# Width-8 attention: scores and shifted scores as paired 64-row tiles

## The chip, the cores and the metric

The kernel runs on one core of a Trainium2 chip. The metric is the device time of one execution in microseconds. TensorE multiplies matrices, VectorE and ScalarE work on what it leaves in PSUM, GpSimd works on SBUF alone, and SyncE issues the DMAs.

## The reference

A network of four layers on x of 16 batches x 256 tokens x 128 features. Each layer adds an attention and then a feed-forward part, each on a layer norm of x. Three of the parts are attentions with 16 heads of width 8, and only they are touched here: the attention of layer 1, the four experts of layer 2's feed-forward part, and the rotary attention of layer 3. Cut to what matters:

```python
# layer 1: 16 batches, one set of weights
q, k, v = split(x @ W_qkv + b_qkv)               # heads of width 8
attn = softmax(einsum('bqhe,bkhe->bqhk', q, k)) / sqrt(128)
x = x + einsum('bihv,bvhd->bihd', attn, v) @ W_out + b_out
# layer 2, for each of 4 experts: keys of tokens that the router
# did not give to the expert are masked, the result is gated
att = softmax(where(valid, einsum('bqhd,bkhd->bhqk', q, k) * 0.5, -1e9))
out += gate[e] * ((att @ v) @ wo[e] + bo[e])
# layer 3: q and k turned by a rotary table, scores * 8 ** -0.5
```

## The kernel before, in words

`attention8` (L287) does one such attention. A *job* is one batch with one set of weights: 16 jobs in layer 1 (stage a1), 64 in layer 2 (a2, masked, four experts per batch), 16 in layer 3 (a3, rotary). The stages between them (layer norms, the 64-wide attention of layer 0, feed-forward parts, a Fourier attention) are not touched.

Queries and keys of a job are projected in float32 and split into three bfloat16 parts each; the parts are written to a scratch in DRAM and read back as *stacks*: for each head a column of 48 rows (six products of parts) in `stackq` and `stackk`, so that one bfloat16 matmul gives the float32-like score. Row 64 carries the mask, rows 96 and 97 the negated row maximum, as two bfloat16 parts.

Each head is computed twice. `scores` (L435) contracts 65 rows and gives query x key; VectorE takes the row maxima (`maxima`, L627). The maxima are negated and split on GpSimd (`split_max`), transposed on TensorE (`turn_max`), copied by ScalarE (`copy_max`) and sent by DMA into the stack (`max_rows`), in two halves of eight heads. `shifted` (L447) then contracts 98 rows and gives key x query less the maximum; ScalarE takes the exponential (`exponential`, L557), and `prob_values` (L460) multiplies with the values, four heads side by side in 32-column tiles, in float32. The result has a column of ones for the denominator; it is copied, transposed (`turn_output`), divided on VectorE (`normalise`), transposed again (`turn_y`) and projected (`project_out`).

All engines run the same software pipeline (`pipeline`, L276): a *step* has 16 slots, one per head, and in the step of job n, TensorE does the scores of job n+1 and the shifted scores of job n, slot by slot; projections for job n+3 stand at the end of the step. Both kinds of score have two PSUM banks each (`psS`, `psT`), so that a head waits for the maximum or the exponential of two heads before. Two more banks are shared in turn by everything else, in the order that `misc_uses` gives. The order on each engine is that of its `step` function. SyncE's DMAs stand in one queue in program order.

```python
for t in range(2):                                   # scores, L443
    mm = pe.matmul(psS[h % 2][:, t * SEQ:(t + 1) * SEQ], stackq[0:MASK_ROW + 1, b, h, t * P:(t + 1) * P],
                   stackk[0:MASK_ROW + 1, b, h, :], start=True, stop=True)
```

The 64-wide attention (L806 on) is not changed, but it has score matmuls of two heads at `tile_position=(64 * h, 0)`, each on 64 rows of the array (L822, L826).

## Time and profile before

| | |
|---|---|
| median of 3 runs | 2939.5 us (2938.18 to 2943.69) |
| the profiled execution | 2944.34 us, span 2942.6 us |
| TensorE busy | 2582.3 us (88%) |
| VectorE, ScalarE, GpSimd busy | 1958.5, 1577.3, 490.1 us |
| mean granted TensorE clock | 0.934 |
| stages a1, a2, a3 | about 700 to 980, 1320 to 2410, 2450 to 2740 us |
| values, 128x256, VectorE (L638) | 425 ns, x96 |
| x with gate, 128x128, VectorE (L659) | 346 ns for most, two per job |
| statistics, VectorE (L114) | 283 ns, two per batch |
| maxima on GpSimd, 128x16 (L730, L732, L734) | 252, 217, 252 ns, each twice per job |
| parts on GpSimd, 128x512 (L720, L722) | 610, 1156 ns, each once per job |

The engines' busy times overlap; each share is of the span. A matmul's duration in the timeline contains its way through the array: where matmuls follow each other, the distance between their starts is what each costs. A float32 product is in the records as two matmuls, and "x16" counts records. A line in the DMA queue's timeline is the issue of a DMA, not its transfer.

### The profile page before, as it was taken

What the parts mean: (1) busy time and instruction counts of PE and PEld (TensorE: products, weight loads), DVE (VectorE), ACT (ScalarE), POOL (GpSimd) and SP (SyncE); (2) the same over time, 40 slices, a digit from 0 to 9 for tenths busy, and PEclk for the clock granted to TensorE, in tenths of its full rate; (3) what the DMA queues carried; (4) which work ended last, traced back from release to release, by engine and by line L of the source; (5) the groups of instructions that cost most, each with busy time, mean ns of one, the idle gap of its engine ahead of it and who ended that gap; (6) DMA issues with size and microseconds to landing.
All of it is one profiled execution on the core that took longest, in us unless ns stands there. A gap on an engine that the chain in (4) does not pass through costs nothing. (4 is left out here: it accounts for less than half of the span.)

```text
span 2942.6 us, 71873 instructions
## 1 busy us (share of the span) xinstructions
PE 2582.3 (88%) x21177; PEld 1696.7 (58%) x21177; DVE 1958.5 (67%) x4869; ACT 1577.3 (54%) x3823; POOL 490.1 (17%) x1071
## 2 busy tenths in 40 slices
PE   5999999796999776649999999999999977999798
PEld 3777777553666444426666666666666644666454
DVE  6666666645878457737787777877778755888211
ACT  2555555423777422226777776777777753666310
POOL 2111111101221000002221222222222203332000
PEclk9999999996999887758999999999999987999899
DMA  4000000001322000002222222222222202222001
GB/s 128 1 0 0 0 0 0 1 1 44 77 70 72 1 1 0 0 17 76 73 72 71 71 75 69 71 73 71 72 71 71 75 25 62 70 66 66 1 0 29
DMA packets 123330, 128.37 MB, mean 44 GB/s; under 512 B 17402, under 2 KB 102222, under 8 KB 123215
## 3 DMA queue, kind: packets, MB, share of 16 engines
q1 hardware_dynamic: 123214, 126.94, 16.0%
q8 instruction: 60, 0.98, 0.1%
q14 instruction: 56, 0.45, 0.1%
HBM read 85.36 MB, written 39.88 MB: 43 GB/s over the span
## 5 line engine op out<-in xcount | busy, mean ns | idle before, releaser
L631 DVE TENSOR_REDUCE a_rowmax<-a_psS 128x2 f32<-128x512 f32 x1536 | 996.0, 685 | 303.9 <-PE a_psS L443 284.1
L561 ACT ACTIVATE a_probs<-a_psT 128x512 f32<-128x512 f32 x1536 | 882.4, 595 | 332.5 <-PE a_psT L455 305.2
L443 PE MATMUL a_psS<-stackk,stackq 65*128 65x256 bf16 x3072 | 607.8, 280 | 103.8 <-DMA stackk<-mask_dram 54.9
L455 PE MATMUL a_psT<-stackq,stackk 98*128 98x256 bf16 x3072 | 593.6, 275 | 14.3 <-ACT a_probs L561 4.7
L443 PEld LDWEIGHTS a_psS<-stackk,stackq 65*128 65x128 bf16 x3072 | 237.2, 98 | 335.0 <-DVE a_rowmax L631 180.2
L469 PE MATMUL a_psO<-a_probs,values 128*32 128x256 f32 x6144 | 414.5, 388 | 0.0
L455 PEld LDWEIGHTS a_psT<-stackq,stackk 98*128 98x128 bf16 x3072 | 275.9, 98 | 115.1 <-ACT a_probs L561 54.0
L893 ACT ACTIVATE a_probs<-a_psS,a_negmax 128x256 f32<-128x256 f32 x256 | 121.2, 473 | 257.0 <-DVE a_negmax L917 257.0
L469 PEld LDWEIGHTS a_psO<-a_probs,values 128*32 128x32 f32 x6144 | 161.0, 109 | 148.3 <-issue 72.1
L730 POOL TENSOR_SCALAR a_negmax<-a_rowmax 128x16 bf16<-128x16 f32 x192 | 48.5, 252 | 984.5 <-DVE a_rowmax L631 982.7
L569 ACT ACTIVATE a_oT<-a_psO 128x256 f32<-128x256 f32 x384 | 145.6, 379 | 46.2 <-PE a_psO L469 46.2
L220 PE MATMUL n_turned<-identity,n_xn 128*128 128x128 f32 x256 | 70.0, 433 | 101.3 <-DVE n_xn L195 98.7
L478 PE MATMUL a_shared<-identity,a_oT 128*128 128x128 f32 x768 | 147.5, 273 | 4.4 <-ACT a_oT L569 4.4
L800 POOL TENSOR_TENSOR a_vr<-a_v,a_rsum 128x256 f32<-128x256 f32 x128 | 78.4, 612 | 372.3 <-DVE a_rsum L927 372.3
L575 ACT ACTIVATE a_negmaxT<-a_shared 16x256 bf16<-16x256 bf16 x192 | 71.5, 372 | 104.5 <-PE a_shared L485 99.0
L1098 DVE TENSOR_SCALAR mlp_h<-mlp_b,s 128x512 f32<-128x512 f32 x32 | 24.0, 751 | 140.3 <-PE mlp_b L1067 86.0
L220 PEld LDWEIGHTS n_turned<-identity,n_xn 128*128 128x128 f32 x256 | 45.7, 217 | 123.7 <-DVE n_xn L195 87.7
L1067 PE MATMUL mlp_b<-mlp_h,k 128*128 128x512 f32 x256 | 114.6, 592 | 0.0
L722 POOL TENSOR_TENSOR a_parts<-a_rest,a_parts 128x512 bf16<-128x512 f32 x96 | 111.0, 1156 | 17.8 <-POOL a_parts L720 17.8
L916 DVE TENSOR_REDUCE a_negmax<-a_psS 128x1 f32<-128x256 f32 x256 | 107.5, 420 | 5.7 <-issue 3.9
L927 DVE RECIPROCAL a_rsum<-a_sums 128x4 f32<-128x4 f32 x128 | 22.8, 178 | 127.0 <-ACT a_probs L895 127.0
L478 PEld LDWEIGHTS a_shared<-identity,a_oT 128*128 128x128 f32 x768 | 94.9, 140 | 13.0 <-ACT a_oT L569 7.2
(192 smaller groups left out, 4140.4 us busy)
## 6 DMA issues: line engine op xcount, KB each, us to landing
a_scratch<-a_parts SPq DMA_DIRECT2D x96, 384.0 KB, 2.8
stackq<-a_scratch SPq DMA_DIRECT2D x192, 96.0 KB
stackk<-a_scratch SPq DMA_DIRECT2D x192, 96.0 KB
stackq<-a_scratch SPq DMA_DIRECT2D x192, 64.0 KB
stackk<-a_scratch SPq DMA_DIRECT2D x192, 64.0 KB
stackq<-a_scratch SPq DMA_DIRECT2D x192, 32.0 KB
stackk<-a_scratch SPq DMA_DIRECT2D x192, 32.0 KB
stackq<-a_negmaxT SPq DMA_DIRECT2D x384, 4.0 KB
```

Source lines behind the costliest of these rows:

```text
L220: t = pe.transpose(turned[b][:, k * D:(k + 1) * D], xn[:, b, k, :], m.identity[:, :])
L443: mm = pe.matmul(psS[h % 2][:, t * SEQ:(t + 1) * SEQ], stackq[0:MASK_ROW + 1, b, h, t * P:(t + 1) * P], stackk[0:MASK_ROW + 1, b, h, :], s ...
L455: mm = pe.matmul(psT[h % 2][:, t * SEQ:(t + 1) * SEQ], stackk[0:MAX_ROW + 2, b, h, t * P:(t + 1) * P], stackq[0:MAX_ROW + 2, b, h, :], sta ...
L469: mm = pe.matmul(psO[g % 2][SLOT * j:SLOT * (j + 1), 0:SEQ], values[:, s.parity(off), t, 4 * g + j, :], probs[:, g % 2, j, t * SEQ:(t + 1) ...
L478: mm = pe.transpose(ps[:, t * P:(t + 1) * P], oT[:, g % 2, t * P:(t + 1) * P], m.identity[:, :])
L561: act.activation(probs[:, h // 4 % 2, h % 4, :], psT[h % 2][:, :], ACT.Exp, scale=w.exp_scale).then_inc(exp_done, 1)
L569: act.activation(oT[:, g % 2, :], psO[g % 2][:, 0:SEQ], ACT.Copy).then_inc(oT_ready, 1)
L631: dve.tensor_reduce(rowmax[:, s.parity(1), h, :], psS[h % 2][:, :].rearrange("p (t k) -> p t k", t=2), AX_X, ALU.max).then_inc(max_done, 1)
L722: pool.tensor_tensor(parts[:, :, 2, :], rest[:, :, :], parts[:, :, 1, :], ALU.subtract).then_inc(parts_ready, 1)
L893: act.activation(probs[:, a, h, 0:SEQ], psS[a][h][:, 0:SEQ], ACT.Exp, bias=negmax[:, a, 2 * h:2 * h + 1], accum_out=sums[:, a, 2 * h:2 * h ...
L916: dve.tensor_reduce(negmax[:, a, 2 * h:2 * h + 1], psS[a][h][:, 0:SEQ], AX_X, ALU.max, negate=True)
L1067: mm = pe.matmul(banks1[c % 2][:, :], w.k1[:, k, c * P:(c + 1) * P], h0[:, s.parity(0), k, :], start=(k == 0), stop=(k == CH - 1))
```

## The change

The stacks of a head now take 51 of 64 rows (48, the mask, two of the maximum), and heads 0-3 and 8-11 lie on rows 0 to 63, the others on rows 64 to 127. So a score matmul uses one half of the array's rows, and the shifted matmul issued beside it is of a head in the other half: in unit u of a step TensorE does head u's scores of job n+1 and the shifted scores of head u+4 of job n-1 (or head u-12 of job n), which are 28 units behind their scores. One wait for both engines stands ahead of the four matmuls.

The maxima of all 16 heads are split, transposed, copied and sent at once, by two DMAs. The stacks are held for four jobs (before: two) and loaded by twelve DMAs, of eight heads each, queries ahead of the maxima and keys behind them; the mask row is one DMA for both groups. The probabilities of all 16 heads are kept; the values are placed so that two blocks of four heads add into one PSUM bank, in columns 0-8 and 9-17 of a head's 32, and there are two output copies and four output transposes per job in place of four and eight. Queries and keys are copied out of PSUM by ScalarE with their bias; GpSimd does the whole split, and in the rotary attention the two products with the table as well, which VectorE did before. The pipeline starts one step earlier and ends one step later.

```diff
 HEADS = 16
 HD = 8
 SLOT = 32
-BF_ROWS = 48
-MASK_ROW = 64
-MAX_ROW = 96
+PAIRS = HEADS // 2
+GROUP_ROWS = 64
+MASK_ROW = 48
+MAX_ROW = 49
+ZERO_ROW = 51
+LEAD = 4
 EXPERTS = 4
...
+    jobs, unroll, first = BATCHES * weights, 4, 4
+    plan = Plan(jobs, weights, unroll, first, rounds=(jobs - LEAD - first) // unroll, drain=2)
+    plan.misc_uses = [("qk", 3)] + ([("qk2", 3)] if rotary else []) + [("o", -2), ("m", 0), ("y", -2), ("out", -2), ("v", 0)]
...
+        def place(h):
+            return h // 4 % 2, 4 * (h // 8) + h % 4
+        def shifted_head(u):
+            return (-1, u + 4) if u < 12 else (0, u - 12)
...
+            def max_rows(s):
+                wait_taken_alone(sp, s, "m", 0, sp_passed)
+                if s.known(0, 1):
+                    wait_alone(sp, shifted_ready, s.n(0, HEADS), sp_passed)
+                for g in range(2):
+                    r = GROUP_ROWS * g + MAX_ROW
+                    sp.dma_start(stackq[r:r + 2, s.quarter(0), :, :], negmaxT[HEADS * g:HEADS * (g + 1), :]).then_inc(maxrow_ready, 16)
+            def save(s):
+                wait_alone(sp, parts_ready, s.n(3, 1, 1), sp_passed)
+                if s.known(3, 2):
+                    wait_alone(sp, stack_ready, s.n(2, stack_inc), sp_passed)
+                sp.dma_start(scratch[s.parity(3)].rearrange("qk part p t -> p qk part t"),
+                             parts[:, :, :, :]).then_inc(parts_saved, 16)
+            def stacks(s, qk):
+                b = s.quarter(2)
+                if qk == 0:
+                    wait_alone(sp, parts_saved, s.n(2, 16, 16), sp_passed)
+                    if s.known(2, 1):
+                        wait_alone(sp, stack_ready, s.n(2, stack_inc), sp_passed)
+                    if s.known(2, 4):
+                        wait_alone(sp, shifted_ready, s.n(-2, HEADS, HEADS), sp_passed)
+                src = scratch[s.parity(2)].rearrange("qk part (g d h) t -> qk part g d h t", g=2, h=PAIRS)
+                for g in range(2):
+                    for repeats, part, row in ((3, 0, 0), (2, 1, 24), (1, 2, 40)):
+                        rows = slice(GROUP_ROWS * g + row, GROUP_ROWS * g + row + 8 * repeats)
+                        if qk == 0:
+                            sp.dma_start(stackq[rows, b, :, :], src[0, part, g, :, :, :].unsqueeze(0).to_broadcast([repeats, HD, PAIRS, SEQ])).then_inc(stack_ready, 16)
+                        else:
+                            sp.dma_start(stackk[rows, b, :, :], src[1, 0:repeats, g, :, :, :]).then_inc(stack_ready, 16)
+                if masked and qk == 1:
                     row = m.mask_dram[s.batch(2), s.expert(2)]
+                    sp.dma_start(stackk[MASK_ROW:P:GROUP_ROWS, b, :, :],
+                                 row.unsqueeze(0).unsqueeze(0).to_broadcast([2, PAIRS, SEQ])).then_inc(stack_ready, 16)
+            def step(s):
+                if s.has(2):
+                    stacks(s, 0)
                 if s.has(0):
+                    max_rows(s)
                 if s.has(2):
+                    stacks(s, 1)
+                if s.has(3):
+                    save(s)
...
+            def scores_part(s, u, t):
+                i, pr = place(u)
+                r, b = GROUP_ROWS * i, s.quarter(1)
+                return pe.matmul(psS[u % 2][:, t * SEQ:(t + 1) * SEQ], stackq[r:r + MAX_ROW, b, pr, t * P:(t + 1) * P],
+                                 stackk[r:r + MAX_ROW, b, pr, :], start=True, stop=True, tile_position=(r, 0))
+            def shifted_part(s, u, t):
+                off, h = shifted_head(u)
+                i, pr = place(h)
+                r, b = GROUP_ROWS * i, s.quarter(off)
+                return pe.matmul(psT[u % 2][:, t * SEQ:(t + 1) * SEQ], stackk[r:r + ZERO_ROW, b, pr, t * P:(t + 1) * P],
+                                 stackq[r:r + ZERO_ROW, b, pr, :], start=True, stop=True, tile_position=(r, 0))
+            def score_pair(s, u):
+                off, h = shifted_head(u)
+                if s.has(1):
+                    if u == 0:
+                        pe.wait_ge(stack_ready, s.n(1, stack_inc, stack_inc))
+                    if s.known(1, 1) or u >= 2:
+                        pe.wait_ge(max_done, s.n(1, HEADS, u - 1))
+                if s.has(off):
+                    if h == 0:
+                        pe.wait_ge(maxrow_ready, s.n(0, 32, 32))
+                    if s.known(off, 1) or h >= 2:
+                        pe.wait_ge(exp_done, s.n(off, HEADS, h - 1))
                 for t in range(2):
+                    if s.has(1):
+                        a = scores_part(s, u, t)
+                        if t == 1:
+                            a.then_inc(scores_ready, 1)
+                    if s.has(off):
+                        b = shifted_part(s, u, t)
+                        if t == 1:
+                            b.then_inc(shifted_ready, 1)
+            def prob_values(s, k):
+                half, i = k // 2, k % 2
+                if k == 0:
+                    wait_taken(pe, s, "v", -1)
+                pe.wait_ge(exp_done, s.n(-1, HEADS, 4 * k + 4))
+                if i == 0 and s.known(-1, 1):
+                    pe.wait_ge(oT_ready, s.n(-1, 2, half - 1))
                 for t in range(2):
                     for j in range(4):
+                        mm = pe.matmul(psO[half][SLOT * j:SLOT * (j + 1), 0:SEQ], values[:, s.parity(-1), t, 8 * i + 4 * half + j, :],
+                                       probs[:, 4 * k + j, t * SEQ:(t + 1) * SEQ], start=(t == 0 and i == 0), stop=(t == 1 and i == 1),
                                        tile_position=(0, SLOT * j), skip_group_check=True)
                 mm.then_inc(pv_ready, 1)
...
+            def turn_output(s):
+                pe.wait_ge(oT_ready, s.n(-2, 2, 2))
+                ps, full = fill(s, "o", -2)
                 for t in range(2):
+                    for half in range(2):
+                        c = (2 * t + half) * P
+                        mm = pe.transpose(ps[:, c:c + P], oT[:, half, t * P:(t + 1) * P], m.identity[:, :])
...
+                for u in range(HEADS):
+                    score_pair(s, u)
+                    if u == 0 and s.has(3):
                         project_qk(s, "qk", w.wq, w.wk)
                         if rotary:
                             project_qk(s, "qk2", w.wq2, w.wk2)
+                    if u == 2 and s.has(-2):
+                        turn_output(s)
+                    if u % 4 == 3 and s.has(-1):
+                        prob_values(s, u // 4)
+                    if u == 4 and s.has(0):
+                        turn_max(s)
+                    if u == 6 and s.has(-2):
+                        turn_y(s)
+                    if u == 9 and s.has(-2):
+                        project_out(s)
+                    if u == 12 and s.has(0):
+                        project_v(s)
...
+            def copy_qk(s, kind, which):
+                ps, taken = wait_full(act, s, kind, 3)
+                if which == 0 and s.known(3, 1):
+                    if rotary:
+                        act.wait_ge(turned_ready, s.n(3, 3))
+                    else:
+                        act.wait_ge(rest_ready, s.n(3))
+                e = s.expert(3)
+                for k in range(2):
+                    bias = w.rot_bias[:, 2 * which + k:2 * which + k + 1] if rotary else (w.bq, w.bk)[k][:, e:e + 1]
+                    c = act.activation(raw[:, which, k, :], ps[:, k * SEQ:(k + 1) * SEQ], ACT.Identity, bias=bias)
+                c.then_inc(taken, 1)
+            def exponential(s, u):
+                off, h = shifted_head(u)
+                if not s.has(off):
+                    return
+                act.wait_ge(shifted_ready, s.n(off, HEADS, h + 1))
+                if h % 4 == 0 and s.known(off, 1):
+                    act.wait_ge(pv_ready, s.n(off, 4, h // 4 - 3))
+                act.activation(probs[:, h, :], psT[u % 2][:, :], ACT.Exp, scale=w.exp_scale).then_inc(exp_done, 1)
...
+                for u in range(HEADS):
+                    if u == 0 and s.has(-2):
+                        copy_oT(s, -2, 1)
+                    if u == 5 and s.has(0):
+                        copy_max(s)
+                    if u == 7 and s.has(-2):
                         copy_yT(s)
+                    exponential(s, u)
+                    if u == 1 and s.has(3):
+                        copy_qk(s, "qk", 0)
+                        if rotary:
+                            copy_qk(s, "qk2", 1)
+                    if u == 8 and s.has(-1):
+                        copy_oT(s, -1, 0)
...
+            def normalise(s):
+                ps, taken = wait_full(dve, s, "o", -2)
+                if s.known(-2, 1):
+                    wait_taken(dve, s, "y", -3)
+                o = ps[:, :].rearrange("p (t h c) -> p t h c", t=2, c=SLOT)
+                for i in range(2):
+                    r = dve.reciprocal(rden[:, i, :, :], o[:, :, :, 9 * i + HD])
+                r.then_inc(rden_ready, 1)
+                dve.wait_ge(rden_ready, s.n(-2, 1, 1))
+                for i in range(2):
+                    of = slice(D // 2 * i, D // 2 * (i + 1))
+                    u = dve.tensor_tensor(y[:, :, of].rearrange("p t (h d) -> p t h d", d=HD), o[:, :, :, 9 * i:9 * i + HD],
+                                          rden[:, i, :, :].unsqueeze(3).to_broadcast([P, 2, 8, HD]), ALU.mult)
+                u.then_inc(taken, 1)
...
+                    if u == 3 and s.has(-2):
+                        normalise(s)
+                    if u == 10 and s.has(-2):
+                        add_output(s)
+                    if u == 11 and s.has(-2) and s.expert(-2) == weights - 1:
+                        output_stats(s)
+                    if u == 13 and s.has(0):
                         write_values(s)
...
+            def turn(s):
+                for which in range(2):
+                    wait_taken_alone(pool, s, ("qk", "qk2")[which], 3, pool_passed)
+                    pool.tensor_tensor(raw[:, which, :, :], raw[:, which, :, :], w.tables[:, which, :, :], ALU.mult).then_inc(turned_ready, 1)
+                wait_alone(pool, turned_ready, s.n(3, 3, 2), pool_passed)
+                if s.known(3, 1):
+                    wait_alone(pool, rest_ready, s.n(3), pool_passed)
+                pool.tensor_tensor(turned[:, :, :], raw[:, 0, :, :], raw[:, 1, :, :], ALU.add).then_inc(turned_ready, 1)
+                wait_alone(pool, turned_ready, s.n(3, 3, 3), pool_passed)
             def split(s):
                 if rotary:
+                    turn(s)
+                    whole = turned[:, :, :]
                 else:
+                    wait_taken_alone(pool, s, "qk", 3, pool_passed)
+                    whole = raw[:, 0, :, :]
+                if s.known(3, 1):
+                    wait_alone(pool, parts_saved, s.n(3, 16), pool_passed)
+                pool.tensor_copy(parts[:, :, 0, :], whole).then_inc(high_ready, 1)
+                wait_alone(pool, high_ready, s.n(3, 1, 1), pool_passed)
+                pool.tensor_tensor(rest[:, :, :], whole, parts[:, :, 0, :], ALU.subtract).then_inc(rest_ready, 1)
+                wait_alone(pool, rest_ready, s.n(3, 1, 1), pool_passed)
                 pool.tensor_copy(parts[:, :, 1, :], rest[:, :, :]).then_inc(middle_ready, 1)
+                wait_alone(pool, middle_ready, s.n(3, 1, 1), pool_passed)
                 pool.tensor_tensor(parts[:, :, 2, :], rest[:, :, :], parts[:, :, 1, :], ALU.subtract).then_inc(parts_ready, 1)
+            def split_max(s):
+                wait_alone(pool, max_done, s.n(0, HEADS, HEADS), pool_passed)
+                if s.known(0, 1):
+                    wait_taken_alone(pool, s, "m", -1, pool_passed)
+                for i in range(2):
+                    mx = rowmax[:, s.parity(0), :, :].rearrange("p (c g j) t -> p g t c j", c=2, g=2)[:, i, :, :, :]
+                    high = negmax[:, :, i, 0, :].rearrange("p t (c j) -> p t c j", c=2)
+                    last = pool.tensor_scalar(high, mx, -1.0, None, ALU.mult)
+                last.then_inc(negmax_step, 1)
+                wait_alone(pool, negmax_step, s.n(0, 2, 1), pool_passed)
+                for i in range(2):
+                    mx = rowmax[:, s.parity(0), :, :].rearrange("p (c g j) t -> p g t c j", c=2, g=2)[:, i, :, :, :]
+                    high = negmax[:, :, i, 0, :].rearrange("p t (c j) -> p t c j", c=2)
+                    dif = maxdif[:, :, 8 * i:8 * i + 8].rearrange("p t (c j) -> p t c j", c=2)
+                    last = pool.tensor_tensor(dif, mx, high, ALU.add)
+                last.then_inc(negmax_step, 1)
+                wait_alone(pool, negmax_step, s.n(0, 2, 2), pool_passed)
+                pool.tensor_scalar(negmax[:, :, :, 1, :], maxdif[:, :, :].rearrange("p t (g h) -> p t g h", g=2), -1.0, None, ALU.mult).then_inc(negmax_ready, 1)
+            def step(s):
+                if s.has(0):
+                    split_max(s)
+                if s.has(3):
                     split(s)
+                if s.has(4):
                     tokens(s)
```

## Rows read from the trace of the kernel before

**Rows 1.** A window: length, busy us of PE PEld DVE ACT POOL, clock, DMA.
```profile
1700.00:1750.00 50.00, 46.63 (x478) 30.86 (x476) 38.73 (x86) 36.19 (x75) 10.69 (x27) 1.00 0.26 72
```

**Rows 2.** Timeline, TensorE, one middle-attention job: start, us, line, tiles, shapes, records [idle <-releaser].
```profile
1701.52 0.39 PE L443 MATMUL a_psS<-stackk,stackq 65*128 65x256 bf16 x2 [0.53 <-DMA stackk<-mask_dram]
...
1702.25 0.38 PE L455 MATMUL a_psT<-stackq,stackk 98*128 98x256 bf16 x2
1702.47 0.38 PE L478 MATMUL a_shared<-identity,a_oT 128*128 128x128 f32 x2
...
1703.01 0.38 PE L455 MATMUL a_psT<-stackq,stackk 98*128 98x256 bf16 x2
1703.33 1.07 PE L469 MATMUL a_psO<-a_probs,values 128*32 128x256 f32 x16
1704.33 0.39 PE L443 MATMUL a_psS<-stackk,stackq 65*128 65x256 bf16 x2
...
1708.39 0.61 PE L431 MATMUL a_shared<-l_wv,a_xcur 128*128 128x128 f32 x4
1708.84 0.38 PE L443 MATMUL a_psS<-stackk,stackq 65*128 65x256 bf16 x2
```

**Rows 3.** Timeline, VectorE, in the job of rows 2.
```profile
1702.04 0.69 DVE L631 TENSOR_REDUCE a_rowmax<-a_psS 128x2 f32<-128x512 f32 x1 [1.40 <-PE a_psS L443]
...
1703.43 1.28 DVE L631 TENSOR_REDUCE a_rowmax<-a_psS 128x2 f32<-128x512 f32 x2
1704.62 0.20 DVE L647 RECIPROCAL a_rden<-a_shared 128x8 f32<-128x8 f32 x1
...
1705.00 1.28 DVE L631 TENSOR_REDUCE a_rowmax<-a_psS 128x2 f32<-128x512 f32 x2
```

**Rows 4.** Timeline, TensorE: the query projections of two jobs, 60 steps apart.
```profile
1350.66 0.60 PE L425 MATMUL a_shared<-a_xcur,l_wq 128*128 128x256 f32 x2
...
2355.51 0.60 PE L425 MATMUL a_shared<-a_xcur,l_wq 128*128 128x256 f32 x2
```

**Rows 5.** Timeline, TensorE, in the 64-wide attention.
```profile
204.78 0.70 PE L822 MATMUL a_psS<-a_qT,a_kT 64*128 64x256 f32 x4
205.31 0.39 PE L826 MATMUL a_psS<-a_qT,a_kT 64*128 64x128 f32 x4
```

**Rows 6.** Timeline, TensorE, in the rotary attention.
```profile
2600.74 0.33 PE L502 MATMUL a_shared<-l_bo_parts,ones_bf 128*128 128x128 bf16 x3
...
2601.63 0.38 PE L443 MATMUL a_psS<-stackk,stackq 65*128 65x256 bf16 x2
...
2617.96 0.33 PE L502 MATMUL a_shared<-l_bo_parts,ones_bf 128*128 128x128 bf16 x3
```

**Rows 7.** Timeline, ScalarE, in the job of rows 2.
```profile
1702.23 1.80 ACT L561 ACTIVATE a_probs<-a_psT 128x512 f32<-128x512 f32 x3 [0.35 <-PE a_psT L455]
```

**Rows 8.** Timeline, SyncE's DMA queue: ahead of rows 2, of rows 9 and rows 10.
```profile
1695.18 0.45 SPq L379 DMA_DIRECT2D stackk<-a_scratch  x1
...
1697.19 0.29 SPq L379 DMA_DIRECT2D stackk<-a_scratch  x1
1697.70 0.72 SPq L382 DMA_DIRECT2D stackk<-mask_dram  x1
1698.62 1.36 SPq L366 DMA_DIRECT2D stackq<-a_negmaxT  x2
...
1797.91 0.72 SPq L382 DMA_DIRECT2D stackk<-mask_dram  x1
...
2393.10 1.31 SPq L366 DMA_DIRECT2D stackq<-a_negmaxT  x2
```

**Rows 9.** Timeline, TensorE: the shifted head that waited for the maxima issued at 2393.10.
```profile
2395.58 0.39 PE L455 MATMUL a_psT<-stackq,stackk 98*128 98x256 bf16 x2 [0.33 <-DMA stackq<-a_negmaxT]
```

**Rows 10.** Timeline, TensorE: another step of the middle attention.
```profile
1802.36 0.39 PE L443 MATMUL a_psS<-stackk,stackq 65*128 65x256 bf16 x2 [1.15 <-DMA stackk<-mask_dram]
...
1804.20 1.81 PE L469 MATMUL a_psO<-a_probs,values 128*32 128x256 f32 x16
```

More of the change, by code:

```diff
@@ L262, in use @@
         step = self.at + off - uses[mine][1]
-        n = sum(0 <= at + o < self.plan.jobs for at in range(-3, step) for _, o in uses)
+        n = sum(0 <= at + o < self.plan.jobs for at in range(-LEAD, step) for _, o in uses)
         n += sum(0 <= step + o < self.plan.jobs for _, o in uses[:mine + 1])
@@ L276, in pipeline @@
 def pipeline(engine, plan, step):
-    for at in range(-3, plan.first):
+    for at in range(-LEAD, plan.first):
         step(Step(plan, at, None))
@@ L359, in _ @@
             if clear_mask:
-                sp.dma_start(stackk[MASK_ROW:MASK_ROW + 1, :, :, :], stackk[BF_ROWS:BF_ROWS + 1, :, :, :]).then_inc(mask_cleared, 16)
-            def max_rows(s, off, half):
-                wait_taken_alone(sp, s, f"m{half}", off, sp_passed)
-                for part in range(2):
-                    sp.dma_start(stackq[MAX_ROW + part:MAX_ROW + part + 1, s.parity(off), 8 * half:8 * half + 8, :],
-                                 negmaxT[8 * part:8 * part + 8, half, :]).then_inc(maxrow_ready[half], 16)
@@ L428, in project_v @@
             def project_v(s):
[L429 removed]
+                ps, full = fill(s, "v", 0)
                 for t in range(2):
[L431 to L432 removed]
+                    mm = pe.matmul(ps[:, t * D:(t + 1) * D], xcur[:, s.quarter(0), t * P:(t + 1) * P],
+                                   w.wv[:, s.expert(0), :], start=True, stop=True)
@@ L496, in project_out @@
             def project_out(s):
-                wait_taken(pe, s, "y", -1)
-                ps, full = fill(s, "out", -1)
-                e = s.expert(-1)
+                wait_taken(pe, s, "y", -2)
+                ps, full = fill(s, "out", -2)
+                e = s.expert(-2)
                 for t in range(2):
@@ L616, in rotary_half @@
-            def rotary_half(s, kind, which):
-                ps, taken = wait_full(dve, s, kind, 3)
-                if which == 0 and s.known(3, 1):
-                    dve.wait_ge(qk_summed, s.n(3))
-                for k in range(2):
-                    t = dve.scalar_tensor_tensor(out=turned[:, which, k, :], in0=ps[:, k * SEQ:(k + 1) * SEQ],
-                                                 scalar=w.rot_bias[:, 2 * which + k:2 * which + k + 1], in1=w.tables[:, which, k, :],
-                                                 op0=ALU.add, op1=ALU.mult)
-                t.then_inc(taken, 1)
```

333 lines of the change are left out of this document (78 added, 255 removed).

## The prediction

> **What bounds the kernel now.** I read the windows first, then the timeline of TensorE over one job, then those of VectorE, ScalarE and the DMA queue in the same stretch. The width-8 attentions fill three stages of 16, 64 and 16 jobs; the change touches nothing else. In the middle one TensorE is busy 46.6 of 50 us at clock 1.00, VectorE 38.7, ScalarE 36.2 [rows 1]. Busy shares don't settle it, so look at starts: nearly every TensorE group starts when the streaming of the one before is over. A head's two shifted matmuls take 0.22 us (1702.25 to 1702.47), and so do its score matmuls; VectorE's next maximum could come every 0.60 (two and the start of the next operation are 1.19 apart). TensorE is the bound, with one short wait per job, on the mask row's DMA at the first head: 0.53 here [rows 2, 3]. Over 60 jobs the mean step is (2355.51 - 1350.66)/60 = 16.75 us [rows 4].
>
> **Do two 64-row tiles run side by side?** The 64-wide attention has such a pair. Four 64-row records of 256 columns (two heads) take 205.31 - 204.78 = 0.53 us [rows 5]; in turn they would take 0.88. Less a mode switch of 0.10 they took 0.43, the time of two. I price the new pair of a score and a shifted head at 0.22 (now 0.44); the bound on the other side is 0.44.
>
> **TensorE's own time after, per job.** 16 pairs x 0.22 = 3.52. A block of probabilities times values still starts its records over 1.00, of which 0.86 is streaming and about 0.12 the way out of the mode; the way in costs 0.32 - 0.22 = 0.10 [rows 2]. Four blocks x 0.86 = 3.44. Output transposes 4 x 0.11 = 0.44 (8 now); values 0.45 (1708.39 to 1708.84) [rows 2]; queries and keys, twice the columns, 0.87; maxima 0.21, y 0.22; output projection 0.88 (2600.74 to 2601.63) [rows 6]. Together 3.07. What is added is switches: all but the pairs now stands in another mode, ten excursions at 0.22 to 0.26, 2.4 us (1.0 now). Sum **12.4 us** against 16.75.
>
> (The Trainium skill, "TensorEngine Tiling", Key Properties, says that a change of the tiling mode drains the engine, which speaks against this change, and gives no price. Rows 2 agree that it costs something; were it free, TensorE's sum would be 2.4 us less.)
>
> **VectorE after:** 16 x 0.60, a normalising of twice the 0.38 that one takes now (1704.62 to 1705.00 [rows 3]), values 0.42, x 0.52, statistics 0.14: 11.5 us. The rest of the split goes to GpSimd, beside other work: two 128x512 operations more, 0.61 and 1.16 in the table ahead, and three in the rotary stage.
>
> **A walk through the step.** Pair u waits for the maximum and the exponential of unit u-2. VectorE starts 1702.04 - 1701.52 = 0.52 after a first score matmul behind a switch, 0.43 without it, and its maximum lasts 0.69 [rows 2, 3]; so pair u comes 0.74 or more after the start of maximum u-2. Exponentials, 0.60 each [rows 7], bind seldom. With TensorE's extras behind units 0, 2, 3, 4, 6, 7, 9 and 11 and VectorE's behind 3 and 10, pairs 0 to 11 start at 0, 1.34, 1.56, 2.51, 3.84, 4.52, 5.09, 5.78, 7.11, 7.33, 8.68, **9.04**; pair 12 could at 10.37, pair 15 at 12.46, and the next step at 13.79. If nothing else waited, that step of 13.8 would win 3 us per job.
>
> **The wait that takes its place.** Now look at SyncE's queue. max_rows waits for shifted_ready at 16 times the step's number: all shifted heads of the jobs before. Those of job n-1 end in unit 11 of step n, because the shifted heads are 28 slots behind. So the two maxima DMAs, whose data are ready at about 5 us, are held until pair 11 is done, and two things stand behind them:
> - Head 0's shifted matmul, in unit 12, needs the maxima. Now they are there 2395.58 - 2393.10 = 2.48 us after the first issue, which TensorE waited for [rows 8, 9].
> - The key stacks (six DMAs) and the mask row of the job whose scores begin the next step are queued behind.
>
> The sum from pair 11: 9.04, the matmul's end and the queue's wake 0.43 + 0.2, two maxima DMAs 1.36 + 0.1 [rows 8], six key stacks 2 x (0.45 + about 0.4 + 0.29) and gaps, 2.5: the mask row is issued at 13.6. From its issue to TensorE's start it takes 1701.52 - 1697.70 = 3.82 in one step now and 1802.36 - 1797.91 = 4.45 in another [rows 2, 8, 10]. I take 4.1, between the two: pair 0 starts at **17.7**. Unit 12 starts at 9.67 + 2.5 = 12.2 and not 10.37, and TensorE is through with its step at about 15.9. It then idles 2 us. The stages without a mask end the queue with a 32 KB stack 0.3 earlier, and land about the same.
>
> Bounds: TensorE alone gets to pair 11 in 8.5; with 3.8 of landing that is a step of 16.9. With 4.45 and wider maxima rows at twice the issue time it is 19.5.
>
> **The clock.** A wait of 1.15 us ahead of the first head, and the next block lasts 1.81 and not 1.07: the clock went from 2.4 to 1.2 GHz for a while [rows 2, 10]. A step of that kind is about 1.8 us longer. Most idles of this length pass without it. After, each step has two idles of 1.8 to 2 us. At a fall in two steps of ten on the part before pair 11, 0.4 us: **18.1 us** per step.
>
> In the rotary stage the second projection costs 0.87 more, and the output transposes of unit 2 now use the bank of the first projection, which ScalarE copies only behind exponential 1, at about 4.1 us. Pair 11 comes 2.3 later: 20.4 against 17.2 now (2600.74 to 2617.96 [rows 6]).
>
> **Ends of a stage.** N jobs had N-1 full steps. After: N-3 full ones, one that waits for no stacks (15.9), a first one without shifted heads (12) and 12 heads behind the last (12 x 0.60 [rows 7] and a block, 9). The start waits for twelve stack DMAs and not six and for one more GpSimd pass: 4 per stage.
>
> **Sum.** 64 jobs: 61 x 18.1 + 15.9 + 21 - 63 x 16.75 = 86. 16 jobs: 13 x 18.1 + 36.9 - 15 x 16.75 = 21. Rotary: 13 x 20.4 + 18.2 + 21 - 15 x 17.2 = 46. With 12 for the starts, 165 us more. The profiled execution took 2944.3 (span 2942.6 and 1.7 around it) and would take 3109; against the median of the runs, 2939.5, it is 3104.5, so **3105 us**. With steps of 17.2 to 19.4, 87 of them, its own range is 3025 to 3220.
>
> **Rivals.**
> *The queue keeps up.* If the held DMAs are off the path (landing much sooner than rows 8 to 10 show), engines set the step: 13.8, and 16.1 in rotary: (18.1 - 13.8) x 87 + 3 x 2.1 = 380 less, 2725 us, **faster**. It decides where the mask row lands under 2.7 us after its issue, as then the step is under 16.75; against it are rows 8 to 10, and that TensorE waits on this DMA today.
> *The clock falls at each idle.* Pairs 0 to 3 and their extras then run at 1.2 GHz in every step: 1.4 us more than allowed, 87 steps: 122, 3227 us. For it: two idles per step. Against: most single idles of today pass. (The skill's page "TensorE: Matmul & The Clock Gate", Part 1, has idleness throttle the clock and activity release it; this case's rows 10 agree with the first.)
> *The pairs run in turn.* Then part of the change doesn't do what it says: eleven pairs cost 0.22 more each before pair 11, 2.4, of which 0.6 is covered by VectorE's waits: +1.8 x 87 = 157, 3262 us. Against it: rows 5.
> *A short landing.* With 3.8 us and no fall the step is 17.4: 0.7 x 87 = 61 less, 3044 us; this is the lower part of my own range.
>
> **Chances.** The forecast with its short landing 72%, clock 10, in turn 4, queue keeps up 8, and 6 for causes that I don't see, half of them near or under the old time. Faster by over 0.2% (about what a measurement of this kernel can tell): 0.09; within: 0.02; slower: 0.89. The range takes in the clock: 2990 to 3250.
>
> **What would show it.** In the waits of TensorE, a DMA ahead of the scores of each unit 0 and ahead of the shifted head of each unit 12, 2 us each; in the DMA queue's timeline, both maxima DMAs start some 0.6 us behind pair 11 and the key stacks right behind them. Score and shifted matmuls start within 10 ns of each other. Projections of queries and keys lie 18.1 us apart (20.4 in rotary). I am wrong in the method if steps are under 16.75, or if unit 0 waits for VectorE and not for a DMA.

## The result, and the profile after

The change makes the kernel slower: 3523.4 us median (3510.48 to 3528.57) against 2938.8 (2935.35 to 2943.69) on the same chip, a ratio of 1.198 [1.196, 1.201]. The prediction had 3105 with a range to 3250: the direction was right, and 418 us are missing from the sum. No rival reached it either; the highest, pairs that run in turn, had 3262. The profiled execution took 3525.7 us, span 3523.9, at a mean clock of 0.772 (0.934 before).

The window that answers to [rows 1] (busy us of PE PEld DVE ACT POOL, clock, DMA):

```profile
1700.00:1750.00 50.00, 37.44 (x336) 16.97 (x332) 26.89 (x55) 23.38 (x48) 11.72 (x26) 0.71 0.20 63
```

No engine is near full: TensorE's 37.4 of 50 us are partly at half clock. Query projections 50 steps apart answer to [rows 4]: (2566.57 - 1462.86)/50 = 22.07 us a step, 16.75 before. Eight steps in the rotary stage are 24.03 each ([rows 6]: 17.2).

```profile
1462.86 1.22 PE L443 MATMUL a_shared<-a_xcur,l_wq 128*128 128x256 f32 x2
...
2566.57 1.22 PE L443 MATMUL a_shared<-a_xcur,l_wq 128*128 128x256 f32 x2
...
2999.24 1.22 PE L443 MATMUL a_shared<-a_xcur,l_wq 128*128 128x256 f32 x2
...
3191.49 1.22 PE L443 MATMUL a_shared<-a_xcur,l_wq 128*128 128x256 f32 x2
```

TensorE in one step of the middle stage, from pair 11 to unit 0 of the next step (start, us; in brackets the idle time ahead):

```profile
2003.69 0.28 PE L456 MATMUL a_psS<-stackk,stackq 49*128 49x256 bf16 x1
2003.70 0.28 PE L463 MATMUL a_psT<-stackq,stackk 51*128 51x256 bf16 x1
2003.81 0.27 PE L456 MATMUL a_psS<-stackk,stackq 49*128 49x256 bf16 x1
2003.82 0.27 PE L463 MATMUL a_psT<-stackq,stackk 51*128 51x256 bf16 x1
2004.02 1.07 PE L499 MATMUL a_psO<-a_probs,values 128*32 128x256 f32 x16
2007.02 0.28 PE L456 MATMUL a_psS<-stackk,stackq 49*128 49x256 bf16 x1 [1.94 <-DMA stackq<-a_negmaxT]
...
2010.46 1.93 PE L499 MATMUL a_psO<-a_probs,values 128*32 128x256 f32 x16
2014.33 0.37 PE L456 MATMUL a_psS<-stackk,stackq 49*128 49x256 bf16 x1 [1.94 <-DMA stackk<-mask_dram]
```

and SyncE's queue in the same step, to set beside [rows 8]:

```profile
2004.22 1.43 SPq L382 DMA_DIRECT2D stackq<-a_negmaxT  x2
2005.71 3.76 SPq L407 DMA_DIRECT2D stackk<-a_scratch  x6
2009.69 0.60 SPq L410 DMA_DIRECT2D stackk<-mask_dram  x1
```

Read together they are the predicted wait: score and shifted matmuls start 10 ns apart; the maxima go out 0.53 us behind pair 11; TensorE idles 1.94 us ahead of unit 12 and again ahead of unit 0, each time until a DMA. The waits from 1500 to 2700 us say the same of all 54 steps (total, times, longest), and the half-clock stretch shows in a window (clock is the third last column):

```profile
PE a_psS L456 <- DMA stackk<-mask_dram: 126.6, 55, 3.8
PE a_psS L456 <- DMA stackq<-a_negmaxT: 98.0, 53, 2.2
```
```profile
2008.00:2018.00 10.00, 7.68 (x48) 3.40 (x48) 3.60 (x8) 3.27 (x7) 1.55 (x6) 0.50 0.26 85
2022.00:2026.00 4.00, 3.65 (x46) 2.07 (x44) 3.31 (x6) 3.29 (x9) 1.16 (x1) 1.00 0.04 14
```

### The profile page after: what moved, and what is told of

Its sections match the earlier page's. It is cut to its first block and busy times, and to the rows that moved or that the text cites. A ratio compares the mean times of both kernels' runs of the same rounds, so it can differ in the third digit from the quotient of the medians.

```text
span 3523.9 us, 67965 instructions
## 1 busy us (share of the span) xinstructions
PE 2756.9 (78%) x20601; PEld 1488.9 (42%) x20601; DVE 1838.2 (52%) x4360; ACT 1469.6 (42%) x3583; POOL 656.3 (19%) x1183
## 5 line engine op out<-in xcount | busy, mean ns | idle before, releaser
L456 PE MATMUL a_psS<-stackk,stackq 49*128 49x256 bf16 x3072 | 673.5, 324 | 506.9 <-DMA stackk<-mask_dram 158.4
L463 PE MATMUL a_psT<-stackq,stackk 51*128 51x256 bf16 x3072 | 676.0, 326 | 6.3 <-ACT a_probs L584 3.4
L456 PEld LDWEIGHTS a_psS<-stackk,stackq 49*128 49x128 bf16 x3072 | 214.5, 102 | 991.8 <-issue 424.8
L499 PE MATMUL a_psO<-a_probs,values 128*32 128x256 f32 x6144 | 534.6, 479 | 0.0
L463 PEld LDWEIGHTS a_psT<-stackq,stackk 51*128 51x128 bf16 x3072 | 213.4, 103 | 39.1 <-issue 18.0
L443 PE MATMUL a_shared<-a_xcur,l_wq 128*128 128x256 f32 x224 | 134.1, 702 | 30.8 <-POOL a_xcur L703 26.2
L726 POOL CAST a_parts<-a_raw 128x512 bf16<-128x512 f32 x80 | 48.9, 611 | 489.8 <-ACT a_raw L574 489.8
L590 ACT ACTIVATE a_oT<-a_psO 128x256 f32<-128x256 f32 x192 | 73.1, 381 | 127.0 <-PE a_psO L499 127.0
L444 PE MATMUL a_shared<-a_xcur,l_wk 128*128 128x256 f32 x224 | 118.7, 634 | 0.0
L510 PE MATMUL a_shared<-identity,a_oT 128*128 128x128 f32 x384 | 95.1, 395 | 15.3 <-ACT a_raw L574 13.8
```

The costliest lines, as they stand in the source:

```text
L443: pe.matmul(ps[:, 0:SEQ], wq[:, s.expert(3), :], xc, start=True, stop=True)
L444: pe.matmul(ps[:, SEQ:2 * SEQ], wk[:, s.expert(3), :], xc, start=True, stop=True).then_inc(full, 1)
L456: return pe.matmul(psS[u % 2][:, t * SEQ:(t + 1) * SEQ], stackq[r:r + MAX_ROW, b, pr, t * P:(t + 1) * P], stackk[r:r + MAX_ROW, b, pr, :], ...
L463: return pe.matmul(psT[u % 2][:, t * SEQ:(t + 1) * SEQ], stackk[r:r + ZERO_ROW, b, pr, t * P:(t + 1) * P], stackq[r:r + ZERO_ROW, b, pr, : ...
L499: mm = pe.matmul(psO[half][SLOT * j:SLOT * (j + 1), 0:SEQ], values[:, s.parity(-1), t, 8 * i + 4 * half + j, :], probs[:, 4 * k + j, t * S ...
```

## The experiments

All runs in one table. "Step" is the mean distance of the first score matmuls of two jobs, over the full steps of the middle and of the rotary stage; "clock" is the mean of the profiled execution. The runs were on several chips, on which the kernel before took 2936 to 2944 us; a difference of some 10 us between two rows is within that.

| kernel | us, median | ratio to before | step | clock |
|---|---|---|---|---|
| changed | 3523.4 | 1.198 [1.196, 1.201] | 22.1, 23.9 | 0.772 |
| e1 no hold | 2980.8 | 1.013 [1.009, 1.017] | 16.7, 17.9 | 0.892 |
| e2 hold, maxima last | 3240.3 | 1.101 [1.097, 1.105] | 18.5, 23.4 | 0.820 |
| e3 hold, warm | 3378.1 | 1.148 [1.144, 1.152] | 20.8, 22.5 | 0.919 |
| e4 no hold, pairs in turn | 3293.8 | 1.119 [1.114, 1.124] | 18.7, 24.1 | 0.853 |
| e5 no hold, split queue | 2914.0 | 0.991 [0.989, 0.994] | 15.9, 16.2 | 0.895 |
| e6 no hold, by size | 3022.1 | 1.028 [1.025, 1.031] | 17.0, 18.3 | 0.884 |
| e7 no hold, split, by size | 2940.2 | 0.999 [0.997, 1.001] | 15.9, 17.0 | 0.890 |
| e8 hold, split queue | 3223.7 | 1.095 [1.091, 1.099] | 18.6, 20.9 | 0.820 |
| e9 e5, two semaphores | 2903.4 | 0.988 [0.986, 0.991] | 15.9, 16.2 | 0.898 |
| e10 e9, save early | 2836.3 | 0.965 [0.963, 0.967] | 14.1, 20.4 | 0.909 |
| **e11 e10, late in rotary** | **2776.3** | 0.945 [0.943, 0.947] | 14.1, 16.2 | 0.919 |
| e12 e11, pairs in turn | 3265.5 | 1.109 [1.104, 1.115] | 19.0, 25.1 | 0.838 |
| e13 e11 and the hold | 3256.3 | 1.107 [1.099, 1.116] | 18.9, 21.0 | 0.818 |

Where the time of a step lies, as the mean over 52 steps of the middle stage (jobs 24 to 76) of the starts of the score matmuls. The last column is from the clock records of the same traces: how often the granted clock fell to 0.50 in these 52 steps, and how long it was there per step between units 0 and 11.

| us | 0 to 11 | 11 to 12 | 12 to 15 | 15 to 0 | step | idle at 12, at 0 | falls; us at 0.50 |
|---|---|---|---|---|---|---|---|
| walk, no queue | 9.04 | 1.33 | 2.09 | 1.33 | 13.79 | 0, 0 | |
| e11 | 9.20 | 1.33 | 2.19 | 1.40 | 14.12 | 0, 0.05 | 0; 0 |
| e5 | 9.68 | 2.32 | 2.21 | 1.69 | 15.90 | 0.95, 0 | 18; 1.13 |
| e1 | 10.29 | 1.33 | 2.19 | 2.84 | 16.65 | 0, 1.45 | 35; 2.53 |
| e13 | 10.21 | 3.23 | 2.63 | 2.73 | 18.80 | 1.84, 0.27 | 52; 2.36 |
| changed | 11.45 | 3.24 | 2.59 | 4.74 | 22.02 | 1.84, 2.31 | 52; 5.22 |

The kernel before has one fall in the same steps. Set against e11, what units 0 to 11 take more goes with the time at 0.50: 1.09 us for 2.53 in e1, 1.01 for 2.36 in e13, 2.25 for 5.22 in the changed kernel. In all nine runs with falls there and the pairs side by side it is 0.42 to 0.44 us per us at half clock.

**e1, the hold taken out.**
```diff
-                if s.known(0, 1):
-                    wait_alone(sp, shifted_ready, s.n(0, HEADS), sp_passed)
```


> Left out: max_rows' wait for shifted_ready (the shifted heads of earlier jobs); nothing else. Hold theory (the two maxima DMAs, and behind them the key stacks and the mask, wait in SyncE's queue for unit 11; TensorE idles ahead of units 12 and 0 and its clock falls there): the maxima go out at about 5.2 us of the step, the key stacks at 6.7, with the 3.8 us that six of them take now the mask at 10.7, and with its 4.6 us of landing pair 0 starts at 15.3. No wait ahead of unit 12, a short one ahead of unit 0. Step 15.3 us against 22.1, total (15.3 - 22.1) x 87 = 590 less, some 2930 us; 2760 if the issues are as quick as in the kernel before and engines set the step at 13.8. Engine theory (mode switches and waits for two engines make the step long): over 3300 us, waits for VectorE and ScalarE ahead of the pairs. Clock over 0.9 in the middle stage by the hold theory, near 0.74 by the other.

2980.8 us: 543 of the 585 us go with these two lines. The idle time ahead of unit 12 is gone; the one ahead of unit 0, for the mask row, is still 1.45 us, and the clock fell 35 times in 52 steps, so the step is 16.65 and not the 13.8 of the walk.

**e2, the hold kept, nothing behind it.** SyncE's step becomes query stacks, key stacks, save, maxima.

> The hold stays, but max_rows is put last in SyncE's step, behind the key stacks, the mask and the save. Hold theory: unit 0 no longer waits for a DMA, unit 12 still does (0.5 us of wake and 2.8 of landing behind pair 11). Step: pair 11 at 9.0 to 9.5, unit 12 at 12.5, four units and a block 3.5: 16.0 at full clock, about 19 if the clock falls at the one idle in every step. (16 to 19 - 22.1) x 87: 2990 to 3250 us. If unit 12's wait were harmless and unit 0's the whole cost, under 2800. Engine theory: as after, 3520.

3240 us: inside the range. The stacks are on time (no idle time at unit 0), and the step still is 18.5: of the 22.0, 3.5 us are what stands behind the hold, and the rest stays.

**e3, TensorE kept busy in its two idle times** by 18 and 32 matmuls on 128 rows that add nothing to the result.
```diff
+                warm = {12: 18, 0: 32}.get(u, 0)
+                if warm and s.has(1) and s.has(-1):
+                    pe.wait_ge(exp_done, s.n(off, HEADS, h - 1))
+                    for _ in range(warm):
+                        pe.matmul(psT[0][:, 0:SEQ], stackk[:, b, 0, 0:P], stackq[:, b, 0, :], ...)
```


> The hold stays. In the two idles TensorE gets extra bfloat16 matmuls of 256 columns (operands of a stack that is there, their result overwritten by the shifted head that follows): 18 ahead of the wait of unit 12 (1.9 us), 32 ahead of that of unit 0 (3.4 us). They add work, no wait. Clock theory (the idles cost more than their length because the clock falls in them and units 12 to 3 then run at 1.2 GHz): the clock in the middle stage rises from 0.74 to over 0.95, pair 11 comes at 9.3 and not at 12.1, the step is 9.3 + 0.5 + 1.5 + 4.0 + 4.6 = 19.9 and the total (19.9 - 22.1) x 87 = 190 less, 3330 us: faster with 50 matmuls more per job. If the clock is a bystander: 3520 or more.

145 us faster with more work. Units 0 to 11 take 9.2 us, as in e11, and most steps are 19.6 to 20.4 instead of 22.0: the clock is worth 2.3 us of each. Every fourth step is 22.5 to 25.9. There the program's loop turns (four steps are one pass), and TensorE's sequencer is in the loop's branch for some 3.7 us, 15 times in the run; in no other run does this branch take more than 0.24 us. TensorE idles about 3 us, and the clock falls. Why the branch is long with 50 more matmuls per step isn't shown.

```profile
L286 PEldq COMPARE_BRANCH  x1: 3801/3801/3801, 1732.9 to 1732.9; - x1
```

The 15 branches are 55 us, about what the run is over its expectation of 3330.

**e4, no hold, and the shifted heads 24 slots behind,** so that the two matmuls of a slot use the same 64 rows.
```diff
-            return (-1, u + 4) if u < 12 else (0, u - 12)
+            return (-1, u + 8) if u < 8 else (0, u - 8)
```


> As e1 (no wait in max_rows), and the shifted heads lag 24 units and not 28, so that the two heads of a pair lie on the same 64 rows and can't run side by side. Against e1 it prices the pairing. Hold theory with the side-by-side price of 0.22 us per pair: TensorE's own time rises from 12.4 to 15.9 us; if e1's step is 15.3, set by DMAs, it goes to 16.5 to 17.3, (1.2 to 2.0) x 87 = 100 to 175 us above e1. If the pairs brought nothing (bound elsewhere): e1's time within 1%.

313 us over e1, not 100 to 175. But for the steps in which the clock changes they are of two kinds: 17.1 to 17.5 at clock 1.00, and 29.2 at half clock, five in a row in the middle stage. Windows:

```profile
1600.00:1700.00 100.00, 100.00 (x522) 50.90 (x518) 42.81 (x81) 38.98 (x76) 16.75 (x36) 0.50 0.12 40
1800.00:1900.00 100.00, 95.13 (x906) 55.51 (x904) 71.45 (x143) 62.81 (x128) 29.42 (x56) 1.00 0.22 71
```

In the first, TensorE is busy in 100.00 of 100 us and the clock stays at 1.2 GHz. Busy time alone did not bring it back here; that departs from the Trainium skill, "TensorE: Matmul & The Clock Gate", Part 1, by which sustained activity brings it back. (The same part reports a clock seen stuck at K=1/4 for 50 us and more; here it is at one half, and the score matmuls of a slot start 0.21 us apart instead of 0.11.)

**e5, no hold, and the mask row and half of the key stacks ahead of the maxima.** With e1, SyncE had been idle there.
```diff
+                    stacks(s, 1, (0,))      # mask row, first row group
                     max_rows(s)
-                    stacks(s, 1)
+                    stacks(s, 1, (1,))      # second row group
```


> The kernel without the wait for pair 11, and in SyncE's step the mask row and the three key stacks of the first row group now stand ahead of the maxima; the three of the second group stay behind them. In the kernel without the wait SyncE is idle from 2004.5 to 2007.9 us of its trace, ahead of the maxima, the mask row is issued at 2013.2 to 2013.8, and unit 0 of the next step idles 2.0 us for it and then runs some 6 us at half clock. Theory (what is left over the 14 us that VectorE and ScalarE allow is the queue behind the maxima): 2.4 us of issue move into the idle time, the last stack is issued at about 2011.2, unit 0's idle time goes and with it the fall of the clock; step 14.0 to 14.8 instead of 16.6, 95 steps, so 2750 to 2830 us, granted clock above 0.95. Rival (TensorE's own work or the max and exp chain holds the step at 16 to 16.6): 2950 to 2981. Rival (a stack lands as late as the mask row did, whatever stands last): idle time 0 to 0.5, but the clock falls all the same: 2850 to 2950.

2914 us, 0.9 % faster than the kernel before, and 84 us above the theory's range. The idle time at unit 0 is gone; in its place TensorE idles 0.95 us ahead of unit 12, for the maxima, and the clock still falls (18 times in 52 steps). The time is in the second rival's range (2850 to 2950), but not by its mechanism, which had the idle time at unit 0.

**e6, stacks of one size behind each other.** The two loops in `stacks` change places.

> The kernel without the wait for pair 11, with the two loops of the stacks swapped: stacks of one size follow each other (96, 96, 64, 64, 32, 32 KB) where they ran 96, 64, 32, 96, 64, 32. In the kernel before, a key stack issued right behind a query stack of its size took 0.43, 0.41 and 0.29 us where the query stack took 0.74, 0.66 and 0.32; in the changed kernel, where each differs from the one ahead of it, all take 0.73, 0.62 and 0.43. Theory (an issue is cheaper behind one of the same size): six stacks issue in about 2.9 us (0.73+0.43+0.62+0.41+0.43+0.29) instead of 3.76; the mask row goes out 0.85 us earlier, 95 steps: 2981 minus 80, so 2870 to 2920, and less if the clock falls less. Rival (the price is that of the source's form, cut by halves of 8 heads before and in one piece now): 3.7 us as before and 2970 to 2990.

The theory falls: six stacks issue in 3.61 us, not 2.9; only the second one of 32 KB is cheaper (0.29). The rival had this right, but its time is missed too: 3022 us, 41 over e1. The mask row is used 5.10 us after its issue instead of 4.77 (means of 52 steps), and why is open:

```profile
1996.77 3.61 SPq L405 DMA_DIRECT2D stackk<-a_scratch  x6
2000.59 0.58 SPq L408 DMA_DIRECT2D stackk<-mask_dram  x1
```

e7 has e6's order and a split of its own: the mask row and four stacks (96 and 64 KB) ahead of the maxima, the two of 32 KB behind them. It was expected at 2730 to 2800 us, or within 0.5 % of e5 if the landing sets unit 0, and took 2940, 26 more than e5. The middle step is the same, 15.9; the rotary one is 17.0 for 16.2. The order was not varied alone here.

**e8, the hold kept, the queue split as in e5.**

> The changed kernel with its wait for pair 11 kept, and in SyncE's step the mask row and the three key stacks of the first row group ahead of that wait; the maxima and the three stacks of the second group stay behind it. Theory (the step is pair 11, then what is queued behind it, then the landing): 2.4 us less is queued behind pair 11, so the step is 22.1 - 2.4 = 19.7, and 19 if the clock falls less; 87 steps: 3523 - 210 to 270, so 3250 to 3320. Rival (the idle time ahead of unit 12, for the maxima, takes over what unit 0 gives back, or the half clock goes on to the next unit 12): under 100 us gained, 3430 or more. Rival (the landing of the mask row was the price, and a stack lands in 2 us): 3150 to 3230.

3224 us, 26 below the theory's range and in that of the second rival, but not by its mechanism: where TensorE waits for a key stack (e13), it is still 4.2 us or more behind its issue. What the theory priced too low is the clock: with no idle time at unit 0 (0.02, and the same 1.85 ahead of unit 12) units 0 to 11 take 10.37 us and not 11.45. The step is 18.6, as in e2 (18.5).

**e9, e5 with two semaphores for landed stacks,** for even and odd jobs, so that SyncE's step no longer starts with the landing of the stacks just issued.

> The kernel with the split queue, with two semaphores for landed stacks, one for even and one for odd jobs, so that the stacks of a job wait for the landing of the job two before it and not of the job before it. Theory (SyncE's own round of 9.4 us of issue and 5.5 to 6.1 us of landing sets the 15.9 us step): the queue's step now starts when the save has landed, 4.7 us after its issue at the end of the step: 9.8 + 0.4 + 4.7, some 15.0 us a step; 90 steps by 0.9: 2914 - 80, so 2810 to 2860 us. Rival (the landing wait is not the bound: the save lands no earlier than the stacks, since both stand in the same queue): 2900 to 2920, no change. Rival (the maxima's own chain, pair 11 to the reduced maxima to unit 12, makes the step): 2914 as well, but with the queue's step starting earlier and waiting longer ahead of the maxima.

2903 us, only 11 less, which the difference between the chips could make: the first rival. SyncE's step still starts 5.4 us behind the save, since its first query stack also waits until the save of the parts has landed:

```profile
1997.23 1.88 SPq L415 DMA_DIRECT2D stackk<-a_scratch  x3
1999.45 0.40 SPq L392 DMA_DIRECT2D a_scratch<-a_parts  x1
2004.83 0.74 SPq L413 DMA_DIRECT2D stackq<-a_scratch  x1
```

**e10, e9 with the save ahead of the last three key stacks.**
```diff
+                    save(s)
                     stacks(s, 1, (1,))
-                    save(s)
```


> The last kernel with the save ahead of the three key stacks of the second row group. Theory of the queue: the save goes out up to 1.9 us earlier, when the parts are ready, and the queue's next step starts that much earlier, but the last three stacks are issued up to 1.1 us later: between 2780 and 2860 us, near the last kernel. Rival (the save of 384 KB stands ahead of the last stacks in the DMA queue, and they land 2 us later, at unit 0's cost): 2880 to 3000.

```profile
1998.00 1.34 SPq L386 DMA_DIRECT2D stackq<-a_negmaxT  x2
2000.41 0.41 SPq L392 DMA_DIRECT2D a_scratch<-a_parts  x1
2000.87 1.93 SPq L415 DMA_DIRECT2D stackk<-a_scratch  x3
2003.74 3.79 SPq L413 DMA_DIRECT2D stackq<-a_scratch  x6
```

2836 us, in the theory's range. SyncE's round is broken: the landing of the save (3.3 us to the next step's first stack) now lies beside the issue of three stacks. The middle step is 14.1, without a fall of the clock in the 52 steps. In the rotary stage the parts come later, the save holds the last stacks, and TensorE idles 2.6 us on average ahead of unit 0: 20.4.

**e11, the save early in a1 and a2 and late in the rotary stage.**

> The last kernel (two semaphores, split queue, save ahead of the last three key stacks), with the save behind them again in the rotary stage alone, where the parts are ready later. Theory (in the rotary stage the save waits 3.8 us for its parts with the last stacks behind it, and unit 0 then idles 3.0 us): its steps fall from 20.4 to the 16.2 that they take with the save last; 11 full steps by 4.2 and 5 us of the filling ones: 2836 - 50, so 2775 to 2800 us. Rival (the rotary stage has a bound of its own at 20 once the middle stage ends earlier): 2836.

2776 us, 5.5 % faster than the kernel before, as expected. The window that answers to [rows 1]: more matmuls than before in it, at full clock.

```profile
1700.00:1750.00 50.00, 46.44 (x548) 23.25 (x546) 42.20 (x88) 37.17 (x78) 17.01 (x32) 1.00 0.26 86
```

**e12, e11 with the pairs in turn (e4's edit).**

> The kernel with the save placed by stage, with the shifted scores 24 slots behind instead of 28, so that a pair's two matmuls use the same 64 rows and run one after the other. Theory (side by side a matmul pair takes 0.22 us of TensorE for 0.44 in turn, and TensorE has no slack of 3 us): 12.4 us of TensorE's own work become 12.4 + 16 x 0.22 = 15.9, and with its waits 17.1 to 17.3 a step as in the kernel with the same lag at full clock; 86 steps by 3.1: 265 more than the kernel by stage, 3040 to 3080, if the clock stays at 2.4 GHz; where it falls, steps of 29 as there, and 3150 to 3300. Rival (the pairs hide behind VectorE and ScalarE, which bound at 14): under 50 us more.

489 us more, in the range for a clock that falls (its profiled execution took 3302); at full clock the step is 17.12 against 14.06 (medians), and some stretches stand at half clock with steps of 29.2. The step at full clock is the measure of the pairs: 3.1 us.

**e13, e11 with the hold put back (e1's lines).**

> The kernel with the save placed by stage, with the wait for pair 11 ahead of the maxima put back; only the maxima, the save and three key stacks stand behind it. Theory (the hold costs by itself: idle time ahead of unit 12 of 1.8 us, unit 12 at 13.6 instead of 10.5 with the clock that falls): 14.1 becomes 18.6 as in the changed kernel with the split queue, 87 steps by 4.5: 390 more, 3150 to 3220. Rival (most of the cost was the queue behind the hold): 14.1 + 1.8 + 0.5 = 16.4, 200 more, 2960 to 3020.

480 us more, beyond both: only the maxima, the save and three key stacks stand behind the hold, and it costs 4.7 us a step all the same.

```profile
2013.37 0.28 PE L466 MATMUL a_psS<-stackk,stackq 49*128 49x256 bf16 x1
...
2016.66 0.28 PE L466 MATMUL a_psS<-stackk,stackq 49*128 49x256 bf16 x1 [1.90 <-DMA stackq<-a_negmaxT]
...
2021.89 0.39 PE L466 MATMUL a_psS<-stackk,stackq 49*128 49x256 bf16 x1 [0.54 <-DMA stackk<-a_scratch]
```

By the table: 1.90 between units 11 and 12, and 2.78 elsewhere (1.01, 0.44, 1.33), where TensorE waits for no DMA but 0.22 us more at unit 0. Of these the 1.01 is the lower clock by the rate above; that the rest is too is argued, not measured (the clock is at 0.50 for 6.85 us of each step).

## Why the prediction was right in direction and wrong in size

**Right.** *Pairs side by side*: 0.22 us a pair, and 3.1 us a step against pairs in turn (e11, e12). *The walk*: without a queue in the way, 9.20 to pair 11 and a step of 14.12, where it had 9.04 and 13.79 (e11). *The wait that takes its place*: the hold, both idle times and their releasers; e1 takes 543 us off with it. The rival "the queue keeps up" (2725) describes e11 to 2 %, but it takes four more edits of SyncE's step to get there.

**Wrong: three terms of one sum.** The mechanism was right, and the sizes were not. The step was 22.02, not 18.1. The 3.9 us are:

- *The clock*, the largest: 2.3 us a step (units 0 to 11 take 11.45 and 9.2 at full clock; e3), 0.4 allowed. The prediction failed where it let the fall be as rare as in the kernel before, from "Most idles of this length pass without it". So they do there: of the 12 idle times of 1.03 to 1.51 us in its middle stage one was followed by a fall. The new ones are 1.84 and 2.31, and the clock fell in 52 of 52 steps: after the idle time ahead of unit 12 it is at 0.50 from 2007.3 to 2020.9, over the second idle time and 6.6 us behind it. The rival that had it at each idle (3227) had the mechanism, and priced it at 1.8 us in all, too little.
- *Six key stacks*: 3.76 us and gaps to the mask row's issue, 3.98 in all, for 2.5. I took [rows 8] for their form, 0.45 and 0.29, which are the issues of stacks of 8 of 16 heads behind a query stack. Here they take 0.73, 0.62 and 0.43, as this kernel's query stacks do. In e6, ordered by size, they are but 0.15 us less in all, so the order isn't the reason. +1.5.
- *The landing of the mask row*: 4.64 from issue to TensorE, 4.1 taken; the larger row of rows 8 and 10 (4.45) was the nearer. +0.5.

With 0.16 of the walk and 0.1 back from the queue's wake these make 3.9 (1.85 + 1.5 + 0.55 + 0.16 - 0.1). Over the 74 full steps of the a stages that is 289 us; 3.5 over 13 in rotary 46. The remaining 80 are the *ends of a stage*: behind the last job's unit 0 the first stage runs 57.4 us on (1025.6 to 1083.0; 57.1 and 57.5 in the others), where the kernel before had 30.5 and my terms give 38.7 (30.5 less 16.75, and 15.9 and 9). The terms were right for a kernel without the hold: in e11 this end takes 37.0. What fails is again the clock. It doesn't come back behind the hold's idle time, though TensorE is busy in 38.1 of 40 us. First the changed kernel, then e11's end:

```profile
1042.00:1082.00 40.00, 38.09 (x230) 16.19 (x230) 5.22 (x18) 18.67 (x37) 1.15 (x5) 0.50 0.01 1
```
```profile
942.00:963.00 21.00, 19.40 (x210) 9.40 (x202) 3.58 (x14) 15.16 (x31) 0.00 (x0) 1.00 0.01 3
```

Three stages by 18.7, by 3.4 for a later start, and by 3.8 for the second step (15.8 in the first stage, 12 taken) are 78.

**What stays open.** Which part of the half-clock time is owed to the idle time and which to the pairs' use of the array isn't separated. e11 runs the same pairs at clock 1.00, so the pairs alone don't do it. The length of the idle time alone doesn't either: in e1 idle times of 1.45 us on average go with 35 falls in 52 steps, in the kernel before one of 12 of about that length. Why a stack's issue is dearer now (one piece of 64 rows of the source, or no query stack of its size ahead) was not isolated. Whether e10 needs e9's two semaphores wasn't tried.

## What to carry to other kernels

A wait put into a DMA queue holds everything behind it: list each DMA issued after it, with its issue time in its new form and its landing, and ask who needs the last of them. If the sum leaves the matrix engine idle for about 2 us in every step, price the whole step's work until the clock is back, not the idle time alone. And look at a queue as a loop: its issues, plus the last landing that its next round waits for, are a bound of their own (15 to 16 us in e5), which no engine's busy share shows.

## What the runs showed of the hardware

- The granted clock can stay at 0.50 for 100 us and more with TensorE busy in 100 % of it (e4 from 1600 to 1700 us, e12 from 1500 to 1600; the score matmuls are on 64 of 128 rows in turn), and the same instructions run at 1.00 a few steps on. The same work side by side stays at 1.00 in the 52 steps of e11.
- With the same pairs, one idle time of 1.84 us in each step goes with a fall to 0.50 in 52 of 52 steps (e2, e13), one of 1.45 us on average in 35 (e1), and 0.05 us in none (e11). Each us at 0.50 made units 0 to 11 longer by 0.42 to 0.44 us.
- With 50 more matmuls in each step TensorE's branch at the loop's turn took 3.7 us on average, otherwise at most 0.24 (e3).
- Matmuls added in idle time made the kernel 145 us faster (e3).
- Where TensorE waits for them, the mask row (8 KB, from DRAM, behind six key stacks) is used 4.7 to 5.1 us after its issue (means: changed, e1, e6), the second maxima DMA (8 KB, from SBUF, 0.7 us behind the first one) 2.0 us after (changed, e2, e8, e13).
